# Opening of a Mamba-style block on one core: one norm root per sequence, the second behind the first low parts, and scaling of the down weights behind it

## The reference, cut to what matters

```python
x = fwht(layernorm(x) * SU_ug) / SCALE             # Hadamard transform over 512
h = silu(x @ W_gate.T * s_g) * (x @ W_up.T * s_u)  # 2048 inner features
h = fwht(h * SU_dp) / SCALE                        # Hadamard transform over 2048
x = x0 + 0.5 * (h @ W_down.T * (Wscale_dp * SCALE))
```

## Time and profile before

| what | us |
|---|---|
| median of 3 runs (1642.52 to 1644.57) | 1643.42 |
| the profiled execution: its own time | 1645.84 |
| its span in the trace | 1644.0 |

### The profile page before, as it was taken

The page is one execution under the profiler, slowest core; times in us unless marked ns, Lnnn a source line. Parts: engine busy times, 40 slices in busy tenths (PEclk is TensorE's granted clock), DMA queues, the critical chain, the costliest instruction groups (busy, mean ns, idle before and its releaser), DMA issues.

```text
span 1644.0 us, 25044 instructions
## 1 busy us (share of the span) xinstructions
PE 1621.2 (99%) x9672; PEld 1313.0 (80%) x9672; DVE 1034.7 (63%) x2022; ACT 626.3 (38%) x934; POOL 378.9 (23%) x298
## 2 busy tenths in 40 slices
PE   6999999999999999999999999999999999999999
PEld 3788888878888778888787888877888878888887
DVE  6543445785677877777776768777775684543333
ACT  5333343464333463333454334355333341122111
POOL 1666652012212212122122122122122121000000
PEclk9999999999999999999999999999999999999999
DMA  9745654754444444454445444445444437556763
GB/s 325 275 172 212 231 192 172 263 183 149 164 163 160 144 156 150 151 169 157 143 162 162 158 152 159 157 131 194 156 156 157 156 127 224 167 181 191 215 203 129
DMA packets 252403, 290.46 MB, mean 177 GB/s; under 512 B 14464, under 2 KB 211200, under 8 KB 243072
## 3 DMA queue, kind: packets, MB, share of 16 engines
q1 hardware_dynamic: 252288, 288.88, 53.0%
HBM read 238.51 MB, written 50.33 MB: 176 GB/s over the span
## 4 chain that ended last, share of the span: by engine, by line
PE 74%; DVE 3%; ACT 1%; issue 1%; DMA 0%; SPq 0%; ACTq 0%; DVEq 0%
PE bank L1191 31%; PE bank L1232 14%; PE bank L1147 12%; PE bank L1260 5%; PE bank L1329 3%; PE bank L1300 2%; PE bank L1316 2%; PE bank L1278 2%; PE bank L1288 1%; PE bank L1323 1%; DVE xT L1750 0%; DVE res L1776 0%; DVE m_cv L1792 0%; DVE m_L L1823 0%; DMA cum_stay<-m_aS 0%
## 5 line engine op out<-in xcount | busy, mean ns | idle before, releaser
L1191 PE MATMUL bank<-fxT,wj 128*128 128x512 f32 x1752 | 415.2, 390 | 0.0
L1191 PEld LDWEIGHTS bank<-fxT,wj 128*128 128x128 f32 x1752 | 328.7, 188 | 68.5
L1232 PE MATMUL bank<-m_wd,m_hb 128*128 128x512 f32 x1128 | 278.8, 393 | 0.0
L1232 PEld LDWEIGHTS bank<-m_wd,m_hb 128*128 128x128 f32 x1128 | 209.2, 188 | 44.9 <-issue 2.4
L1544 ACT CAST m_hb<-xn 128x512 fp32r<-128x512 f32 x96 | 59.5, 620 | 452.5 <-DVE xn L1763 452.5
L1147 PE MATMUL bank<-xT,wi 128*128 128x512 f32 x900 | 224.4, 397 | 1.6 <-DVE m_cv L1792 0.5
L1147 PEld LDWEIGHTS bank<-xT,wi 128*128 128x128 f32 x900 | 167.2, 189 | 40.1 <-issue 5.1
L1776 DVE TENSOR_TENSOR res<-bank,res 128x512 f32<-128x512 f32 x192 | 132.5, 690 | 83.0 <-PE bank L1232 80.9
L2099 POOL TENSOR_TENSOR m_L<-m_L,m_GT 128x512 f32<-128x512 f32 x36 | 52.8, 1466 | 434.4 <-ACT m_L L1553 434.4
L1763 DVE SCALAR_TENSOR_TENSOR xn<-bank,sc,xn 128x512 f32<-128x512 f32 x96 | 71.7, 747 | 121.6 <-PE bank L1191 121.5
L1538 ACT ACTIVATE xn<-bank,sc 128x512 f32<-128x512 f32 x96 | 66.1, 689 | 146.3 <-PE bank L1191 140.9
(11 more groups left out here) (224 smaller groups left out, 2317.8 us busy)
## 6 DMA issues: line engine op xcount, KB each, us to landing
wj<-ug_split SPq DMA_DIRECT2D x167, 512.0 KB, 4.2
m_wd<-dn_split SPq DMA_DIRECT2D x48, 1024.0 KB, 4.8
wi<-in_split SPq DMA_DIRECT2D x76, 512.0 KB, 3.2
ug_split<-b_wu SPq DMA_DIRECT2D x8, 2048.0 KB, 14.0
m_wo<-out_split SPq DMA_DIRECT2D x32, 512.0 KB, 4.1
wi<-ug_split SPq DMA_DIRECT2D x25, 512.0 KB, 4.2
in_split<-b_msp SPq DMA_DIRECT2D x20, 512.0 KB, 3.8
raw<-in_wug SPq DMA_DIRECT2D x8, 1024.0 KB, 6.8
```

Of the source, the lines that this page charges most:

```text
L1191: ins = pe.matmul(to[:], w[:, a, k, :], frm[:, b, k, :], start=(k == 0 and i == 0), stop=(k == KH - 1 and i == 2))
L1232: ins = pe.matmul(F[t % 2][:], hb[:, a, j, ck(t)], wd[:, b, j, :], start=(j == 0 and n == 0), stop=(j == 1 and n == 2))
```

## The change

It touches only the opening. The first root covers sequence 0 alone; a second root, for sequence 1, stands on DVE behind the low parts of sequence 0 and group 8. DVE then scales all its remaining groups in one run, groups 10 and 12 first. SP loads x of sequence 0 behind two groups instead of four. PE turns the first weights behind two groups. ACT copies groups earlier in relation to `rows` and the units. POOL waits for the first root before it multiplies groups 2 and 3. The wait of POOL's butterflies for all scaled groups (L435) is not edited.

```diff
 sync:
             fetch(0)
-            for i in range(4):
-                load_group(i)
+            load_group(0)
+            load_group(1)
             sp.dma_start(res[:, 0:TPG, :], xt[:, 0:TPG, :]).then_inc(s_x0, 16)
+            load_group(2)
+            load_group(3)
             sp.dma_start(res[:, TPG:2 * TPG, :], xt[:, TPG:2 * TPG, :]).then_inc(s_x1, 16)
 gpsimd:
             for i in range(4):
+                if i == 2:
+                    pool.wait_ge(s_mv, 1)
                 pool.wait_ge(s_gc, i + 1)
 tensor:
-            for i in range(4):
-                group(i)
+            group(0)
+            group(1)
             for k in range(KH):
                 turn(("ug", 0, k))
-            for i in range(4, 8):
+            for i in range(2, 8):
                 group(i)
 scalar:
-                act.wait_ge(s_mv, max(1, c))
+                act.wait_ge(s_mv, c + 1)
...
-            for i in range(4):
-                group(i)
+            group(0)
+            group(1)
             for k in range(KH):
                 turn(("ug", 0, k))
-            group(4)
-            group(5)
+            for i in range(2, 5):
+                group(i)
             rows(0)
             for t in range(TPG):
                 turn(("x", 0, t))
-            group(6)
-            group(7)
-            group(9)
+            for i in (5, 6, 7, 9, 11):
+                group(i)
             rows(1)
+            group(13)
+            group(15)
             act.wait_ge(s_sc, 16)
...
                 silu(n, 0)
-                if n == 0:
-                    group(11)
-                    group(13)
...
                 silu(n, 1)
-                if n == 0:
-                    group(15)
 vector:
-            for landed, c in ((s_x0, 0), (s_x1, 1)):
-                dve.wait_ge(landed, 16)
-                for t in range(TPG * c, TPG * c + TPG):
-                    own.done(dve.bn_stats(st[:, t, :], res[:, t, :]))
-            run(roots(dve, st, mv, own))
-            bias(0, 2 * TPG)
+            dve.wait_ge(s_x0, 16)
+            for t in range(TPG):
+                own.done(dve.bn_stats(st[:, t, :], res[:, t, :]))
+            run(roots(dve, st[:, 0:TPG], mv[:, :, 0:TPG], own))
+            bias(0, TPG)
             for k in range(KH):
                 turn(("ug", 0, k))
             for t in range(TPG):
                 turn(("x", 0, t))
-            for i in (8, 4, 5, 6, 7, 9):
+            group(8)
+            dve.wait_ge(s_x1, 16)
+            for t in range(TPG, 2 * TPG):
+                own.done(dve.bn_stats(st[:, t, :], res[:, t, :]))
+            run(roots(dve, st[:, TPG:2 * TPG], mv[:, :, TPG:2 * TPG], own))
+            bias(TPG, TPG)
+            for i in (10, 12, 4, 5, 6, 14, 7, 9, 11, 13, 15):
                 group(i)
...
             for n in range(UNITS - 1):
                 keys = unit_turns(n)
-                if n == 0:
-                    for i in range(10, 14):
-                        group(i)
                 for key in keys[0]:
                     turn(key)
-                if n == 0:
-                    group(14)
-                    group(15)
```

## The result

The changed kernel takes 1650.8 us (median of 5 runs, 1648.9 to 1652.54) against 1644.57 us of the kernel before in the same comparison (5 runs, 1642.52 to 1645.58): **6.2 us slower**, ratio 1.0041, 95% interval 1.0026 to 1.0056. The forecast was 1649.5 us, +6.1 against the 1643.42 shown before.

The account below looks back on a forecast made before the run. PE, busy 99% of the span, was taken to bound the kernel, with an equally long chain through SP and DMA. A later read back (4.5) plus low clock (1.6) gave +6.1 us, 1649.5 us; range 1644.0 to 1651.6.

Parts of the forecast that it names:

- The first rows: Sequence 0's statistics, root and rows in the opening: bias ends 3.35 us earlier, and PE gains 3.3 us at up(0, 0).
- The second root: New work of 4.28 us on DVE for sequence 1; PE still about 2.8 us ahead up to there.
- The writes: Down weights on SP's queue: group 4 is scaled 4.75 us later, so the read back holds PE's turn 4.5 us later.
- The clock: PE's granted clock falls behind its pause of some 7 us and costs 1.6 us, bounds nothing to 3.2 us.
- The sum: Behind the stall all is PE's own work, so nothing gives time back: 4.5 + 1.6 = +6.1 us.
- A: Rival: the read back of down_half doesn't hold PE, so its 2.8 us gain reaches the end: 1640.6 us; chance 0.14.
- B: Rival: SP's DMA queue catches up by part, PE stands 1 to 2 us later: 1644.4 to 1647 us; chance 0.10.
- C: Rival: DVE comes even later to its groups or the low clock lasts longer: +8 to +10 us; chance 0.06.
- POOL: POOL's groups 2 and 3 wait for the first root; priced at nothing, covered by 12 us until group 4 is scaled.

Follow-up runs that it names:

- e1: The change, with SP issuing fetch(2) and keep_up(0) behind fetch_down(1) instead of between the writes of the down groups; 1644.65 us against 1644.78 for the kernel before.
- e8: The change, with SP issuing fetch(2) and keep_up(0) right behind the write of group 3; 1642.28 us against 1644.76 for the kernel before.
- e5: The change, with DVE scaling group 4 ahead of groups 10 and 12; 1651.19 us against 1644.76 for the kernel before.
- e11: e8 once more, beside its control on the same chip; 1642.59 us against 1644.03 for the kernel before.
- e3: The kernel before, with SP also waiting for group 10 to be scaled ahead of the write of group 4; 1648.53 us against 1644.78.
- e10: The kernel before, with SP waiting ahead of the write of group 4 until DVE has scaled group 11; 1651.85 us against 1644.03.
- e7: The change without POOL's wait for the first root ahead of groups 2 and 3; 1652.81 us against 1644.76 for the kernel before.
- e2: The kernel before, with SP issuing fetch(2) and keep_up(0) behind fetch_down(1); 1643.72 us against 1644.78.
- e9: The kernel before, with SP issuing fetch(2) and keep_up(0) right behind the write of group 3; 1644.14 us against 1644.03.
- e6: The change, with DVE scaling groups 4 to 7 ahead of the statistics and root of sequence 1; 1643.04 us against 1644.76 for the kernel before.

## Why the prediction was right

- **The first rows.** Forecast: bias at 19.7, `up(0, 0)` at 26.1. Measured 19.3 and 25.60, but everything in this trace starts some 0.15 us earlier. Right. One thing was not in the sum: between the first two groups and the turns of the gate weights PE now waits 0.6 us for DVE's butterflies (0.16 to 0.35 in the experiments), while it still runs at half its later pace: its weight loads are 0.85 us apart, then 0.43, though the column of the granted clock reads 1.00 there. The eight matmuls of the turns took 3.70 us in the change, 4.42 in e1, 4.28 in e8 and 4.78 in e5. It is a loss of up to 1.1 us that differs by execution, and it accounts for e8's first down projection being 2.6 us ahead of before and not 3.1; in e11, where the turns took 3.85, it is 3.2.
- **The second root.** Forecast: bias at 33.1, `up(1, 0)` at 45.4 to 45.9. Measured 32.65 and 45.23. Right.
- **The writes.** Forecast: `fetch(2)` at 35.5, `fetch_down(0)` at 55.1, PE's turn 4.5 us later. Measured 34.84, 54.21 and 3.7 (weight load at 57.95 against 54.27). The mechanism is shown by e3 and e10; the term was 0.8 us too large. Half of that is the earlier DVE chain (group 4 scaled at 34.45, forecast 35.0), the rest the queue, which lost 3.86 us where its start lost 4.15. One reading was wrong and did no harm: the last write was to be issued at about 42.1 in both cases, but the last two went out from 44.35 on, against 40.97 before: SP took 0.9 to 1.2 us for each write behind `keep_up(0)`, though the last group was scaled by 39.8.
- **The clock.** Forecast 1.6 us. Measured 2.4 (11.81 against 9.43, from the first matmul of the turn on). This term was mis-sized. The granted clock stood at 0.50 from 56 to 62.8, and 4.9 us of PE's work fell into that, not about 3; what I had taken over from the earlier trace rows was the length of a low stretch in which PE worked from its start to its end. What counts is how much of it is left when PE resumes, as e7 shows: there the loss was 1.65 us behind a longer pause. The bound of 3.2 us held. Of the 5.67 us only 2.0 remain behind the 3.7, as the two are counted from different places: the first matmul followed its weight load by 0.42 us before and by 0.03 after.
- **The sum.** 4.5 + 1.6 = 6.1 forecast; 3.7 + 2.0 = 5.7 in the trace and 6.2 in the medians. The path, the wait and both terms were there; that the number came out within 0.1 us is luck. The terms were off in opposite directions, the trace of before is up to 0.8 us behind executions with the clock up, and the measured 6.2 has an interval of 4.3 to 9.2 us. The range was also not the sum of its bounds: together they give +3.0 to +8.7 us and not +4 to +8.2.
- **The rivals.** A (the read back does not hold PE) did not come, but e8 and e11 show what it would have been worth: 2.5 and 1.4 us less than their kernel before, where I wrote 2.8. B (the queue catches up) came by 0.3 us. C did not come.
- **POOL.** I priced its wait at nothing. As an added wait that is right, but e7 shows that it earns 2.0 us at the first root and 1.3 us at the first down projection: without it the first root is slowed by POOL. The prediction had not looked at the port.

## What to carry to other kernels

When an engine's wait goes away, look for the chain that was just on time beside it: here a read back with 0.3 us to spare, fed through a DMA queue with a backlog, whose first entry was pushed behind a new block of work. In a queue with a backlog, as here, the first late entry counts and not the last, and moving large transfers without a deadline ahead of the late entry, into an idle stretch, repairs it. When you price a low clock behind a pause, count the work that falls into the low stretch, and look first whether the trace you compare with has one of its own. Put small dependent operations of VectorE and low parts on PE's path where GpSimd is silent.

## What the runs showed of the hardware that I had not expected

- PE's pause of 3.1 us left the granted clock up (e3), those of 4.1, 5.3, 6.3 and 6.6 us brought it to 0.50, 1.2 GHz (e5, e10, the change, e7). Below that the length did not decide it: behind the wait for `xn`, 2.91 us brought it down before, and so did 2.11 us in e10, but 2.28 us in e2 and 2.63 us in e9 did not. The low stretch cost 1.65 to 2.85 us of PE's time behind the long pauses, and the least behind the longest.
- The clock also fell once inside the mixer without a change there (0.50 at 371 to 373 us), in the profiled execution of before and not in that of the change: 1.5 us between the two.
- VectorE operations on 128x4 elements took 1.17 and 1.19 us instead of 0.16 beside GpSimd, and two low parts on 128x512 took 3.49 (before), 4.26 (the change), 4.91 (e1) and 5.42 us (e6) instead of 1.46.
